# Transposes of slot, output, q and k in halves of 64 rows into two PSUM banks, with the slot's transpose one step earlier

## The reference

```
h    = einsum('bct,bcd->bdt', x, style_weights[style])      # 32x32 per sequence, over its 32 tokens
q, k, v = split(clip(h @ w_qkv.T, -8, 8))                   # 512 -> 3 x 512
q, k = layer_norm(q) * w + b, layer_norm(k) * w + b
probs = softmax(q k^T / 4 + alibi + causal)                 # 32 heads of 16
x1   = x + (probs v) @ w_out.T
y    = einsum('bsi,boi->bso', x1, adapter_weights[adapter]) # 512 x 512 per sequence
h2   = relu(y @ up) ** 2
out  = x1 + layer_norm(h2 @ down + (y @ fc1 @ expert) * top2sum(y @ gate) @ fc2)
```

## Time and profile before

| | us |
|---|---|
| median of 3 runs | 1129.94 (1128.02 to 1130.91) |
| profiled execution | 1126.27 |
| its span, first to last instruction | 1124.5 |
| PE busy | 1088.2 (97%) |
| POOL busy | 713.4 (63%) |
| DVE busy | 676.1 (60%) |
| ACT busy | 602.5 (54%) |
| mean granted clock of TensorE, share of full | 0.994 |

### The profile page before, as it was taken

One profiled execution on the slowest core, in us unless ns is written; L12 is line 12 of the kernel. 1 busy time (PEld: TensorE's weight loads), 2 busy tenths in 40 slices (PEclk: granted clock), 3 DMA queues, 4 the chain that ended last, 5 costly groups with the idle time before them and its releaser, 6 DMA issues.

```text
span 1124.5 us, 27403 instructions
## 1 busy us (share of the span) xinstructions
PE 1088.2 (97%) x10996; PEld 890.1 (79%) x10996; DVE 676.1 (60%) x1040; ACT 602.5 (54%) x985; POOL 713.4 (63%) x612
## 2 busy tenths in 40 slices
PE   5999999999999999999999999999999999999994
PEld 3878788888888888888877778787878888787883
DVE  5567666666666667667666245565655565554432
ACT  4466767676767677777776425335161625333220
POOL 4566888788888887878676464556455464533342
PEclk9999999999999999999999999999999999999997
DMA  7125555646464646565567953233514123030101
GB/s 277 41 79 182 171 201 166 202 160 212 158 209 158 214 152 219 172 211 156 201 226 234 375 166 95 85 96 106 113 48 133 59 90 99 29 85 29 47 29 37
DMA packets 95292, 160.77 MB, mean 143 GB/s; under 512 B 46400, under 2 KB 47168, under 8 KB 89792
## 3 DMA queue, kind: packets, MB, share of 16 engines
q1 hardware_dynamic: 79456, 118.16, 32.6%
q0 software_dynamic: 12224, 34.10, 9.5%
q10 hardware_dynamic: 3488, 6.78, 1.7%
HBM read 93.97 MB, written 42.47 MB: 121 GB/s over the span
## 4 chain that ended last, share of the span: by engine, by line
PE 95%; DMA 1%; issue 1%; DVE 1%; POOL 0%; ACT 0%; SPq 0%; DVEq 0%; ACTq 0%; POOLq 0%
PE bank L648 24%; PE pair L832 15%; PE bank L808 15%; PE bank L738 10%; PE bank L688 8%; PE bank L825 8%; PE pair L665 3%; PE bank L696 3%; PE pair L710 3%; PE bank L638 3%; PE bank L723 1%; PE bank L778 1%; PE bank L676 1%; DMA xt<-in_x,tile_rows 1%; PE bank L759 0%
## 5 line engine op out<-in xcount | busy, mean ns | idle before, releaser
L1675 POOL TENSOR_TENSOR w_lo<-w2t,w_hi 128x2048 fp32r<-128x2048 f32 x38 | 174.8, 4600 | 39.6 <-ACT w_hi L994 36.2
L648 PE MATMUL bank<-wqkv_hi,h_hi 128*128 128x512 f32 x384 | 153.9, 401 | 0.2
L648 PE MATMUL bank<-wqkv_hi,h_lo 128*128 128x512 f32 x384 | 150.0, 391 | 0.0
L648 PE MATMUL bank<-wqkv_lo,h_hi 128*128 128x512 f32 x384 | 149.7, 390 | 0.0
L1745 POOL TENSOR_TENSOR u_lo<-act,u_hi 128x512 fp32r<-128x512 f32 x64 | 82.7, 1292 | 103.3 <-ACT u_hi L1187 103.2
L808 PE MATMUL bank<-yT_hi,up_hi 128*128 128x512 f32 x256 | 100.8, 394 | 0.0
L808 PE MATMUL bank<-yT_hi,up_lo 128*128 128x512 f32 x256 | 99.8, 390 | 0.0
L1524 DVE TENSOR_TENSOR act<-act 128x512 f32<-128x512 f32 x59 | 67.0, 1135 | 54.6 <-ACT act L1183 54.6
L808 PE MATMUL bank<-yT_lo,up_hi 128*128 128x512 f32 x256 | 99.6, 389 | 0.0
L832 PE MATMUL pair<-down_hi,u_hi 128*128 128x512 f32 x256 | 99.6, 389 | 0.0
L832 PE MATMUL pair<-down_lo,u_hi 128*128 128x512 f32 x256 | 99.6, 389 | 0.0
(11 more groups left out here) (178 smaller groups left out, 2908.8 us busy)
## 6 DMA issues: line engine op xcount, KB each, us to landing
w2t<-in_w SPq DMA_DIRECT2D x38, 1024.0 KB
vx<-v_hl SPq DMA_DIRECT2D x128, 68.0 KB
x1g<-x_rows SPq DMA_DIRECT2D x32, 256.0 KB, 3.0
kx<-k_hl SPq DMA_DIRECT2D x124, 64.0 KB
x_rows<-x1t SPq DMA_DIRECT2D x31, 256.0 KB
ffn_high<-w_high SPq DMA_DIRECT2D x20, 256.0 KB, 3.6
ffn_low<-w_low SPq DMA_DIRECT2D x20, 256.0 KB, 3.3
stage<-in_wqkv SPq DMA_DIRECT2D x3, 1024.0 KB, 9.4
```

The source lines that it names most:

```text
L648: m = e.matmul(into, a[:, c, :], b[:, n, c, :], start=(c == 0 and k == 0), stop=(c == KC - 1 and k == 2))
L1675: e.tensor_tensor(w2_lo[:, :, :], w2t[:, :, :], w2_hi[:, :, :].bitcast(F32), ALU.subtract).then_inc(d_wlo, 1)
```

## The change: what it does

- The banks 4 and 5, and 6 and 7, become two pairs, `banks45` and `banks67`. A transpose of 128 rows becomes two of 64 rows, rows 0 to 63 into the first bank of a pair and rows 64 to 127 into the second. `half(banks, n)` names half the columns of both banks: slot and output use `banks45`, q and k `banks67` (of the last tile `banks45`). 118 groups of four transposes become groups of eight: 26 slots, 28 outputs, 32 each of q and k.
- `project_v` writes bank 4, `out_project` bank 3 (bank 7 for the last three tiles), `style` bank 6 for tiles 0 and 1, bank 5 for 2 to 4, bank 2 after. `make_route` writes bank 5 for routes 1 to 3.
- `style(i + 1)` moves ahead of the transposes, and these stand directly ahead of the scores.
- `turn_slot`, `slot_in` and `gather_slot` are a step earlier: the slot's rows are gathered in the step in which they are transposed. ACT's `slot_in` stands at the end of the step, DVE's `low_slot` near the head of the next. SP's `store_x1` moves ahead of `spread_v`.
- The waits follow the new sharing of banks. The loop on PE now includes the last step.

The diff, cut:

```diff
-    bank = [psum(f"bank{i}", [P, DM]) for i in range(2, 8)]
+    B2, B3 = (psum(f"bank{i}", [P, DM])[:, :] for i in (2, 3))
+    banks45, banks67 = psum("banks45", [P, 2, DM]), psum("banks67", [P, 2, DM])
     pair = psum("pair", [P, 2, DM])
-    B2, B3, B4, B5, B6, B7 = (b[:, :] for b in bank)
+    B4, B5, B6, B7 = banks45[:, 0, :], banks45[:, 1, :], banks67[:, 0, :], banks67[:, 1, :]
...
-    def k_bank(t):
-        return B4 if t < 3 else B5
+    def half(banks, n):
+
+        return banks[:, :, n * KC * HALF:(n + 1) * KC * HALF].rearrange("p g (c t) -> p g c t", c=KC)
+
+    def by_half(tile):
+
+        return tile.rearrange("p c (g t) -> p g c t", g=ROW_TILES)
+
+    def h_bank(t):
+        return B6 if t < 2 else B5 if t <= SHORT else B2
+
+    def q_banks(t):
+        return half(banks67 if t < T - 1 else banks45, 0)
+
+    def k_banks(t):
+        return half(banks67 if t < T - 1 else banks45, 1)
+
+    turned_values = banks45[:, :, KC * HALF:2 * KC * HALF]
+
+    def value_bank(t):
+        return B2 if t == T - 4 else B6
+
+    def slot_halves(tile):
+
+        return by_half(tile.rearrange("p (c t) -> p c t", c=KC))
+
+    def out_bank(t):
+        return B3 if t <= T - 4 else B7
 
     def route_bank(c):
-        return pair[:, 0, :] if c == 0 else B7
+        return pair[:, 0, :] if c == 0 else B5
...
+                if i >= 5:
+                    store_x1(i - 5)
                 if i >= 4:
                     spread_v(i - 3)
-                if i >= 5:
-                    store_x1(i - 5)
...
-                upto(e, "x1", t - 6)
                 upto(e, "hlo", t - 1)
+                if t > SHORT:
+                    upto(e, "cq", t - 1)
+                elif t == SHORT:
+                    e.wait_ge(s_routec, 2)
                 for c in range(KC):
-                    m = e.matmul(B6[:, P * c:P * c + P], xt[t % XR][:, P * c:P * c + P],
+                    m = e.matmul(h_bank(t)[:, P * c:P * c + P], xt[t % XR][:, P * c:P * c + P],
                                  style_bd[t % 2][:, :, :].rearrange("p j d -> p (j d)"), start=True, stop=True)
...
             def turn_values(t):
                 upto(e, "on", t)
-                upto(e, "olo", t - 1)
-                if t:
-                    e.wait_ge(r_low, min(t, CHUNKS))
+                if t <= T - 5:
+                    upto(e, "cv", t + 4)
+                    upto(e, "olo", t - 1)
+                    if t == 0:
+                        e.wait_ge(s_routec, KC)
+                    else:
+                        e.wait_ge(r_low, min(t, CHUNKS))
+                    if t >= 2:
+                        e.wait_ge(d_tl, t - 1)
+                elif t == T - 4:
+                    e.wait_ge(d_mc, LAST + 1)
+                else:
+                    upto(e, "qlo", T - 2)
+                    upto(e, "klo", T - 2)
+                    upto(e, "olo", t - 1)
                 for b in range(BPT):
-                    m = e.transpose(B4[:, P * b:P * b + P],
-                                    on[:, b, :, :].rearrange("p g d -> p (g d)"), ident)
+                    if t <= T - 5:
+                        for g in range(ROW_TILES):
+                            rows = slice(HALF * g, HALF * g + HALF)
+                            dst = turned_values[:, g, :].rearrange("p (j b q) -> p j b q", j=ROW_TILES, b=BPT)
+                            m = e.transpose(dst[:, :, b, :], on[rows, b, :, :].rearrange("p g d -> p (g d)"),
+                                            ident[rows, rows])
+                    else:
+                        m = e.transpose(value_bank(t)[:, P * b:P * b + P],
+                                        on[:, b, :, :].rearrange("p g d -> p (g d)"), ident)
                 m.then_inc(A["ot"], 1)
 
             def out_project(t):
                 upto(e, "olo", t)
...
                 e.wait_ge(d_x[s % 2], 16 * (s // 2 + 1))
                 if s == 0:
                     e.wait_ge(s_routec, KC)
-                elif s <= LAST:
-                    e.wait_ge(d_tl, s)
+                if s <= LAST:
+                    upto(e, "cv", s + LAG - 1)
+                    upto(e, "olo", s)
+                    e.wait_ge(r_low, min(s + 1, CHUNKS))
+                    if s:
+                        e.wait_ge(d_tl, s)
                 for c in range(KC):
-                    m = e.transpose(into[:, P * c:P * c + P], xg[s % 2][:, P * c:P * c + P], ident)
+                    if s <= LAST:
+                        for g in range(ROW_TILES):
+                            rows = slice(HALF * g, HALF * g + HALF)
+                            m = e.transpose(into[:, g, c, :], xg[s % 2][rows, P * c:P * c + P], ident[rows, rows])
+                    else:
+                        m = e.transpose(into[:, P * c:P * c + P], xg[s % 2][:, P * c:P * c + P], ident)
                 m.then_inc(d_t, 1)
 
             def adapt_slot(s, into):
...
                 if s <= LAST:
-                    upto(e, "cq", min(s + LAG, T - 1))
-                    if s:
-                        e.wait_ge(d_mc, s)
+                    upto(e, "cq", s + LAG)
+                    upto(e, "hlo", min(s + LAG + 1, T - 1))
...
                 e.wait_ge(s_latc, LC)
                 e.wait_ge(s_fc2, 16)
-                if c >= 2:
+                if c:
+                    upto(e, "hlo", min(c + 2, SHORT))
                     e.wait_ge(s_routec, c)
...
+            def banks_free(t):
+                if t == T - 1:
+                    upto(e, "cv", T - 1)
+                    upto(e, "olo", T - 5)
+                    e.wait_ge(d_tl, LAST + 1)
+                    e.wait_ge(r_low, CHUNKS)
+                elif t:
+                    upto(e, "qlo", t - 1)
+                    upto(e, "klo", t - 1)
+                else:
+                    upto(e, "hlo", 1)
 
             def turn_q(t):
-                upto(e, "ck", t + 1)
-                turn_qk(t, qn[t % 2], "qn", B3, "tq")
+                banks_free(t)
+                turn_qk(t, qn[t % 2], "qn", q_banks(t), "tq")
 
             def turn_k(t):
-                if t > 2:
-                    upto(e, "cv", t + 1)
-                turn_qk(t, kn[t % 2], "kn", k_bank(t), "tk")
-
-            for i in range(T - 1):
+                banks_free(t)
+                turn_qk(t, kn[t % 2], "kn", k_banks(t), "tk")
+
+            for i in range(T):
                 if 0 < i < SHORT:
                     style(i + 1)
                 project_q(i)
@@ -890,15 +967,15 @@
                     make_route(i - 1)
                 project_k(i)
                 project_v(i)
-                if i >= LAG:
-                    turn_slot(i - LAG, B7)
+                if SHORT <= i < T - 1:
+                    style(i + 1)
+                if LAG - 1 <= i < T - 1:
+                    turn_slot(i - LAG + 1, half(banks45, 0))
                 if i >= 4:
                     turn_values(i - 4)
                 if i >= 1:
                     turn_q(i - 1)
                     turn_k(i - 1)
-                if i >= SHORT:
-                    style(i + 1)
                 if i >= 2:
                     scores(i - 2)
                 if i >= LAG:
@@ -908,23 +985,8 @@
                 if i >= 3:
                     values(i - 3)
 
-            project_q(T - 1)
-            project_k(T - 1)
-            project_v(T - 1)
-            turn_slot(LAST, B7)
-            turn_values(T - 5)
-            turn_k(T - 2)
-            turn_q(T - 2)
-            scores(T - 3)
-            adapt_slot(LAST, B2)
-            e.wait_ge(d_tl, LAST + 1)
-            turn_qk(T - 1, qn[(T - 1) % 2], "qn", B7, "tq")
-            upto(e, "khi", T - 2)
-            upto(e, "klo", T - 2)
-            turn_qk(T - 1, kn[(T - 1) % 2], "kn", B5, "tk")
-            values(T - 4)
-            out_project(T - 5)
-
+            turn_q(T - 1)
+            turn_k(T - 1)
...
-            def scale_q(t, at):
+            def scale_q(t):
                 upto(e, "tq", t)
+                upto(e, "tk", t)
                 for c in range(KC):
-                    m = e.activation(at[:, P * c:P * c + P], at[:, P * c:P * c + P], ACT.Identity,
+                    m = e.activation(q_banks(t)[:, :, c, :], q_banks(t)[:, :, c, :], ACT.Identity,
                                      bias=qkln[:, KC + c:KC + c + 1], scale=qkln[:, c:c + 1])
                 m.then_inc(A["qT"], 1)
...
-            def low_q(t, at):
+            def low_q(t):
                 upto(e, "qhi", t)
+                upto(e, "khi", t)
                 upto(e, "s", t - 1)
-                e.tensor_tensor(q_lo[:, :, :], at.rearrange("p (c t) -> p c t", c=KC), q_hi[:, :, :],
+                e.tensor_tensor(by_half(q_lo[:, :, :]), q_banks(t), by_half(q_hi[:, :, :]),
                                 ALU.subtract).then_inc(A["qlo"], 1)
 
...
                     divide(i - 4)
+                if i >= LAG:
+                    low_slot(i - LAG, half(banks45, 0))
                 take_q(i)
                 if i < SHORT:
...
```

(25 more changed lines are left out.)

146 lines of the change are left out of this document (81 added, 65 removed).

## The result

| | before | changed |
|---|---|---|
| median of 4 runs each, us | 1128.98 | 1177.72 (1172.26 to 1180.66) |
| profiled span, us | 1124.5 | 1170.5 |
| PE busy, us | 1088.2 | 1087.7 |
| mean granted clock | 0.994 | 0.981 |

The ratio is 1.0425, interval 1.0379 to 1.0471: 49 us slower, where 7 us faster was forecast and the range ended at 1141.

What follows compares the result with a forecast made beforehand. PE, busy 97%, was taken as the bound. Steps 7 to 30 -13.2, beginning +7.5 - 2.1, end 0, gather +0.5, clock +0.3 sum to -7.0: 1129.94 to 1123 us; range 1113 to 1141, forecast's own 1116 to 1129.

Steps and rivals of the forecast that it cites:

- Turn groups: Eight half turns on PE ahead of the scores, side by side: 0.26 us a group, 0.55 us gained per step.
- The two rivals on the pace of half loads: PE's half turns load one after the other (1149 us, chance 0.12), or a pair takes a whole turn's time (1140, 0.05).
- the 107 ns for a half turn: Estimate for PE's half turns from the skill's rule of column loads over 1.2 GHz; by it nothing would be gained.
- All else ... is taken at 0: Everything else, such as evacuations across two banks, was taken to cost 0 beside PE's wide matmuls.
- the 1.80: PE's 1.80 us wait, placed ahead of the last q turn near the loop's end, was forecast to go.
- The gather: Slot rows gathered and wanted in the same step: landing 8.4 to 8.5 in, wanted at 9.25; 0.5 us charged in all.
- the late one: Rival: the slot's gather lands 5.9 rather than 4.2 us after issue, costing 23 us: 1146 us, chance 0.08.
- The beginning: Routes 1 and 2 wait on PE for h's low part, 2.9 (up to 3.4) and 4.4 us: 7.5 lost.
- clock too small: Clock falling in PE's two early stalls, with matmuls behind at half speed: 0 to 4 us, taken as 0.3.
- The end: Loop end: the wait before the last q turn goes, but the last k is turned later; -2 to +2, taken as 0.

Runs made afterwards that it cites:

- three: Changed kernel with the slot's turn behind the output projection, routes 1 and 2 behind the v projection, scores between k and v projections: 1138.95 us, ratio 1.0110.
- slot_late: Changed kernel with the slot's turn moved from the head of the turns to behind the output projection of the same step: 1161.67 us, ratio 1.0314.
- slot_route: Changed kernel with the slot's turn behind the output projection and routes 1 and 2 behind the v projection: 1152.14 us, ratio 1.0216.

## Why the prediction was wrong

**Turn groups (0.26 each, 0.55 a step): right.** Two thirds of 0.27 is 0.18, not 0.19, so the sum should have said 0.25; the runs showed 0.25 to 0.29, and undisturbed steps of 18.21 to 18.38 where 18.2 to 18.3 was named. The two rivals on the pace of half loads fell; so did the 107 ns for a half turn that the Trainium skill's page "TensorE: Matmul & The Clock Gate" leads to: a pair starts every 0.06.

**"All else ... is taken at 0": the failed step.** The prediction took the issue of PE as limited by dispatch and waits alone, asked what a group costs, and not whether the instructions behind it would be there in time. With 472 more instruction pairs in the kernel and turns done in 1.0 us instead of 1.75, PE reaches the end of a block before the next has landed. Price: 20.4 us of stalls in steps 4 to 30, 6.4 of half clock behind some of them, and most of the 8.5 from step 31 on (one stall of 4.79 at 628.23). No rival held it, and the trace of before had shown it: a stall inside the scores at 115.70, and the 1.80 that I booked as one that "goes". That one is a border, and I misread its place: by the earlier trace rows it lies ahead of a matmul of the adapter product (L738), not ahead of the last q turn. That PE stands for its next block is shown. Why it came to that is shown in part: of the 21.6 us in steps 4 to 30, 7.2 follow blocks passed in under 2 us, and 14.4 follow blocks whose transfer began 4.0 to 6.8 behind the border.

**The gather (0.5 charged, the late one at 0.08): wrong in one term.** Store issued 0.53 into the step (named 0.6), landed 3.0 later (3.6), gather landed 4.4 after its issue (4.2); medians of 25 steps. But it was issued at 5.0, not 4.2, since GpSimd, not the store, was last. Its queue in step 10, which began at 197.78:

```profile
198.69 1.10 POOL L1719 DMA_INDIRECT y_rows<-ys,slot_rows  x1 [1.55 <-PE pair L696]
200.09 1.00 POOL L1698 DMA_INDIRECT xt<-in_x,tile_rows  x1 [0.31 <-issue]
...
202.66 1.02 POOL L1713 DMA_INDIRECT xg<-x_rows,slot_rows  x1 [0.30 <-issue]
```

I let its DMAs move forward by the 1.16 of the slot's gather taken out of the step before; the first of them is released by PE's values, 0.9 into the step, so nothing moved. Landing at 9.55 against 9.25 wanted in the middle case, later in the tail: 13.2 us in 17 waits. The late gather was a rival, priced at 23. Its outcome came, but not its reason: it let the landing take 5.9 from issue, and the landing took 4.4; the issue was late.

**The beginning (7.5): waits right, clock too small.** Route 1 and 2 waited 3.5 and 4.5 (named 2.9 to 3.4, and 4.4):

```profile
48.50 3.75 PE L822 MATMUL banks<-fc_sb,latT 128*128 128x512 f32 x4 [3.54 <-DVE h_lo L1456]
```

The clock fell in both, to a mean of 0.82 and 0.92 of the steps, and cost some 4.1 (what is left of the 12.8 beside the waits) where I took 0.3 from a range of 0 to 4.

**The end (0, -2 to +2): wrong**, +8.5. That most of it is the stall at 628.23 is shown by the runs without one there: 551.5 with whole turns, 553.2 with the scores moved, 551.1 in three; with it, slot_late has 558.5 and slot_route 558.8.

Left open: why in the changed kernel the transfers began 2.6 to 6.8 us behind their border wherever it lay among long matmuls, and in the kernel before mostly near it or ahead of it. The runs do vary it (in three the 15 such borders of steps 7 to 30 lie between 0.7 ahead and 3.5 behind, and no stall is left), but always together with the order of PE's work, so its cause and its share of the loss stay open. Had the transfers begun 1.0 behind the border, the three blocks of 6.7 to 7.3 us would have had no stall at all, an estimate from 1.0 + 1.1 + 1.3 = 3.4.

## What to carry to other kernels

Count the instructions of an engine over time, not only its busy time. If 256 of them pass in less than about 3.4 us (medians of the changed kernel: lag 1.0, transfer 1.1, start 1.3), PE can stand at a block's border, at a place that moves from step to step and that the profile calls "issue". Blocks of up to 7.3 us stalled too, where the transfer began late, so read the start of the transfer beside the border, and not the length of the block alone. A change that makes a short, dense stretch denser, or puts two side by side, can pay for it; here it helped to put long matmuls between them. And a wait for nothing, in the profile before, is a reading to explain before it is booked as gone.

## What the runs showed of the hardware

- 48 more instructions a step cost 12 us, 96 cost 35.5: stalls grow faster than the work.
- A stall of 1.7 to 3.4 us can drop TensorE's granted clock to its 1.2 GHz level for the next matmuls, and need not: in the loop it did behind four of nine (behind the one that ended at 151.48 the adapter product's twelve matmuls took 4.83 instead of 2.61 from first to last start), while behind the one of 3.16 that ended at 311.70 they took 2.62.
- Two row tiles of 64 by 128 load and multiply side by side: eight half transposes in fp32 start within 0.19 to 0.24 us.
- PE's instructions come in transfers of 16,384 bytes, one for 256 instructions (92 for 23,734). PE stood at the end of a block until 1.2 to 1.5 us after the next had landed.
